# Attention plus expert-LoRA feed-forward block: value/LoRA column split 384 + 280, denominators in four column strips, token-stage order changed

## The chip, the cores and the metric

The kernel runs on one core of one Trainium2 chip. The metric is the device time of one execution in microseconds (us), lower is better; three runs of the kernel before are shown. The engines are named as in the profile: PE (TensorE), DVE (VectorE), ACT (ScalarE), POOL (GpSimd), SP (SyncE, which only issues DMAs here).

## What is computed

2048 tokens (2 x 1024) of width 512. After a layer norm, two branches are added to the input: linear attention and a gated feed-forward with routed low-rank experts.

```python
xn = layernorm(x)
# attention, 16 heads of 32
Q = elu(xn @ wq.T + bq) + 1;  K = elu(xn @ wk.T + bk) + 1;  V = xn @ wv.T + bv
KV = einsum('bhsd,bhse->bhde', K, V);  K_sum = K.sum(over tokens)
att = (Q @ KV) / (Q . K_sum + 1e-8)            # per head
att = att @ wo.T + bo
# feed-forward: 8 experts, top 2, rank 8, hidden 1376
scores = sigmoid(xn @ W_router); top 2 of (scores + expert_bias); w = their scores / (their sum + 1e-8)
gate = xn @ W_gate + shared LoRA + sum_e w_e * (xn @ A_gate[e]) @ B_gate[e] / 8      # up: the same
out  = (silu(gate) * up) @ W_down + shared LoRA + weighted expert LoRAs
return x + att + out
```

## The kernel before, in words

Every product is made nearly exact by splitting each operand into a rounded high part and the remainder (`_h`, `_l`, type fp32r): `product` issues three matmuls, L1112 to L1114 (high x high, high x low, low x high). Each engine has its own program, written out by hand; the order on an engine is the order of the code, and semaphores are the only link. `tiles` peels the first two and the last two tiles and puts the others into a loop of two tiles per turn.

**Token stage** (16 tiles of 128 tokens, `stage1` on each engine). On PE, for tile t: keys (512 columns, into bank 1), transposes of the normalised tokens of tile t+1 (L1129), transposes of the LoRA rows of tile t-2 (L1147), values (512 columns), then the low-rank inputs and router logits z (152 columns: 64 + 64 expert columns, 8 + 8 shared, 8 router), then keys by values of tile t-1 (L1139, accumulated over two tiles). Twelve matmuls make each of the three products of a tile. DVE, ACT and POOL work the tile up:

- layer norm of tile t+2: DVE statistics (L795, L799), POOL `rstd_of` (L508, L510), DVE `normalise` (xn, L804);
- keys: DVE bias (kb, L866), ACT krelu and kexp (L627, L630), DVE kf (L878);
- routing of tile t-1: ACT rexp (L642), POOL 1 + exp (L529), DVE `compare` (score, biased, gt, eq, L827 to L834), POOL ranks (L532 to L536), DVE `select` (sel, L839), POOL the sum, its inverse and the weights (L539 to L545);
- LoRA rows of tile t-1: DVE `lora_weighted` (zs, zf, L845, L849), ACT `lora_hi` (zst), DVE `lora_lo` (zst, L791);
- z of tile t: DVE copy out of the bank (zraw, L890), which has one buffer; every second tile DVE adds the keys-by-values bank (kvacc, L816).

POOL's loop is `rstd_of(t + 2)` and then `route(t)`, so the rstd of tile t+2 stands behind the routing of tile t-1. The output weight `wo` is split into high and low in tiles 14 and 15, two quarters each.

**Attention stage** (4 groups of 512 tokens): queries, `denominators` (L1223), DVE adds 1e-8 and takes the reciprocal (L964, L966), the reciprocals are split into `rr` and spread over the head's columns by a matmul with `hrow` (`expand`, L1231), and the attention matmuls follow. `denominators` is four matmuls in full fp32, one per 128 columns of Q, each with a 128 x 16 stationary tile `kcur` (key sums, zero off the head's own column); the four accumulate into the same 16 rows of a bank. DVE builds `ksel` once (L1001), POOL copies a batch's part into `kcur` (L565). Rows 0 to 15 of `rr` hold the high parts, rows 32 to 47 the low parts.

**Feed-forward stage** (4 groups x 11 chunks): gate, up and down products. The change does not touch it.

## Time and profile before

| | before |
|---|---|
| median of 3 runs | 725.01 us (724.76 to 725.21) |
| the profiled execution | 723.72 us |
| its span in the trace | 721.9 us |
| PE / PE weight loads busy | 98% / 79% |
| DVE / ACT / POOL busy | 53% / 36% / 17% |
| granted TensorE clock, mean | 1.00 |
| HBM traffic | 72.8 MB, 101 GB/s over the span |

A busy share is an average over three stages with different limits: the token stage lies at about 9 to 150 us of the span, the attention stage at 150 to 262 us, the feed-forward behind it. The start of an instruction is recorded; the end of a matmul is modelled, so consecutive matmuls overlap on paper and their rate is read from start to start.

### The profile page before, as it was taken

To read this page: it belongs to the slowest core of one execution; us is meant where nothing else is said; L and a number is where in the kernel's file an instruction comes from. 1 tells how busy PE (TensorE), PEld (TensorE's weight loads), DVE (VectorE), ACT (ScalarE), POOL (GpSimd) and SP (SyncE) were. 2 spreads that over 40 slices of the span, in tenths; PEclk is the share of its full clock that TensorE was granted. 3 is DMA by queue.
4 is the path that set the end of the run, shared out by engine and by line. 5 is a ranking of instruction groups with operands and counts; after the bars stand their busy time and mean duration, and the time that the engine had idled before them with its cause. 6 is when DMAs were issued, how large, how long until landed. Compare 5 with 4: busy or idle time off the path is not lost.

```text
span 721.9 us, 10024 instructions
## 1 busy us (share of the span) xinstructions
PE 706.6 (98%) x3306; PEld 570.8 (79%) x3306; DVE 380.2 (53%) x715; ACT 260.8 (36%) x402; POOL 123.1 (17%) x293
## 2 busy tenths in 40 slices
PE   7999999998999999999999999999999999999997
PEld 5888888876776767888888888888888888888886
DVE  5666655677666665444336543436534435544434
ACT  4343333563431432333324333324332324323322
POOL 3544455421633632000000000000000000000000
PEclk9999999999999999999999999999999999999999
DMA  7765556235755644100001600001600001300001
GB/s 248 276 199 195 185 189 220 88 146 195 287 183 206 214 166 172 63 0 0 0 11 48 233 0 0 0 0 58 232 0 0 0 0 58 116 0 0 0 0 59
DMA packets 22754, 73.03 MB, mean 101 GB/s; under 512 B 2560, under 2 KB 2816, under 8 KB 20688
## 3 DMA queue, kind: packets, MB, share of 16 engines
q1 hardware_dynamic: 22560, 72.50, 28.3%
q0 software_dynamic: 176, 0.30, 0.3%
q8 instruction: 10, 0.16, 0.1%
q14 instruction: 8, 0.07, 0.0%
HBM read 51.82 MB, written 20.97 MB: 101 GB/s over the span
## 4 chain that ended last, share of the span: by engine, by line
PE 88%; DVE 5%; issue 2%; POOL 2%; ACT 1%; DMA 1%; SPq 0%; DVEq 0%; POOLq 0%
PE bank L1112 18%; PE bank L1113 18%; PE bank L1114 18%; PE bank L1323 17%; PE bank L1298 6%; PE bank L1310 4%; PE bank L1223 2%; PE bank L1139 1%; PE bank L1175 1%; DMA w_raw<-in_wkT 1%; PE bank L1129 1%; PE bank L1147 1%; PE bank L1231 1%; PE bank L1339 0%; PE bank L1341 0%
## 5 line engine op out<-in xcount | busy, mean ns | idle before, releaser
L1112 PE MATMUL bank<-x,up_h 128*128 (+1 forms) x352 | 137.5, 391 | 2.1 <-DVE qf L977 1.2
L1113 PE MATMUL bank<-x,up_h 128*128 (+1 forms) x352 | 137.2, 390 | 0.0
L1114 PE MATMUL bank<-x,up_l 128*128 (+1 forms) x352 | 137.0, 389 | 0.0
L1045 DVE TENSOR_TENSOR hf<-bank,silu 128x512 f32<-128x512 f32 x44 | 30.4, 692 | 162.3 <-issue 142.6
L1112 PEld LDWEIGHTS bank<-x,up_h 128*128 128x128 f32 x352 | 66.1, 188 | 18.7 <-issue 2.1
L595 ACT ACTIVATE hid_h<-hf 128x512 fp32r<-128x512 f32 x44 | 27.8, 632 | 142.9 <-DVE hf L1045 142.9
L1114 PEld LDWEIGHTS bank<-x,up_l 128*128 128x128 f32 x352 | 66.1, 188 | 14.0
L1113 PEld LDWEIGHTS bank<-x,up_h 128*128 128x128 f32 x352 | 66.1, 188 | 13.8
L791 DVE TENSOR_TENSOR up_l<-up_raw,up_h 128x1024 fp32r<-128x1024 f32 x45 | 55.6, 1235 | 31.4 <-ACT up_h L595 31.4
L1323 PE MATMUL bank<-dn_h,hid_h 128*128 128x512 f32 x176 | 69.5, 395 | 0.0
L1323 PE MATMUL bank<-dn_l,hid_h 128*128 128x512 f32 x176 | 69.1, 393 | 0.0
L1323 PE MATMUL bank<-dn_h,hid_l 128*128 128x512 f32 x176 | 68.9, 392 | 0.0
L595 ACT ACTIVATE up_h<-up_raw 128x1536 fp32r (+1 forms) x45 | 66.0, 1474 | 1.5 <-DVE qf L946 1.5
L748 ACT ACTIVATE silu<-bank 128x512 f32<-128x512 f32 x44 | 26.3, 597 | 101.7 <-PE bank L1298 101.5
L1298 PE MATMUL bank<-z,up_h 128*128 128x512 f32 x176 | 54.2, 389 | 0.0
L791 DVE TENSOR_TENSOR hid_l<-hf,hid_h 128x512 fp32r<-128x512 f32 x44 | 30.5, 692 | 33.8 <-ACT hid_h L595 33.8
L595 ACT ACTIVATE dn_h<-dn_raw 128x592 fp32r (+1 forms) x44 | 30.8, 699 | 43.0 <-PE bank L1310 31.4
L791 DVE TENSOR_TENSOR up_h<-up_raw,up_h 64x256 fp32r<-64x256 f32 x90 | 39.5, 439 | 0.6
L791 DVE TENSOR_TENSOR dn_l<-dn_raw,dn_h 128x592 fp32r<-128x592 f32 x44 | 34.1, 775 | 10.4 <-ACT dn_h L595 9.3
L1323 PEld LDWEIGHTS bank<-dn_h,hid_l 128*128 128x128 f32 x176 | 33.0, 188 | 7.6
L1323 PEld LDWEIGHTS bank<-dn_h,hid_h 128*128 128x128 f32 x176 | 33.0, 187 | 7.5
L1323 PEld LDWEIGHTS bank<-dn_l,hid_h 128*128 128x128 f32 x176 | 33.1, 188 | 7.1
(167 smaller groups left out, 1252.6 us busy)
## 6 DMA issues: line engine op xcount, KB each, us to landing
x<-scr_x SPq DMA_DIRECT2D x8, 2048.0 KB, 7.4
up_raw<-in_ffn_up SPq DMA_DIRECT2D x11, 768.0 KB, 5.4
scr_x<-xt SPq DMA_DIRECT2D x16, 512.0 KB, 4.2
xin<-in_x SPq DMA_DIRECT2D x16, 256.0 KB, 5.8
scr_z<-zt SPq DMA_DIRECT2D x16, 256.0 KB, 2.2
x3r<-in_x SPq DMA_DIRECT2D x16, 256.0 KB, 4.0
scr_att<-x3r SPq DMA_DIRECT2D x16, 256.0 KB, 2.1
z<-scr_z SPq DMA_DIRECT2D x4, 1024.0 KB, 4.8
```

The source lines that it names most:

```text
L595: return nc.scalar.activation(dst, src, ACT.Copy)
L748: nc.scalar.activation(silu[:], ps_g[:], ACT.Silu).then_inc(silu_done, 1)
L791: return nc.vector.tensor_tensor(dst, a, b.bitcast(F32), ALU.subtract)
L1045: nc.vector.tensor_tensor(hf[:], ps_u[:], silu[:], ALU.mult).then_inc(h_done, 1)
L1112: nc.tensor.matmul(dst, lh, rh, start=start, stop=False, **kw)
L1113: nc.tensor.matmul(dst, lh, rl, start=False, stop=False, **kw)
L1114: return nc.tensor.matmul(dst, ll, rh, start=False, stop=stop, **kw)
L1129: last = nc.tensor.transpose(ps_xt[:, k * P:(k + 1) * P], xn[:, k * P:(k + 1) * P], ident[:])
L1223: last = nc.tensor.matmul(ps_den[0:HEADS, :], kcur[:, c, :], qf[:, c, :], start=(c == 0), stop=(c == KD - 1))
L1298: last = nc.tensor.matmul(dst[:], up_h[:, s, col:col + P], z4[:, :, a * 2 + b, :], start=False, stop=(b == 1))
L1310: d = nc.tensor.matmul(ps_zd[0:DNR, :], w[:, s, D:], h[:, s, :], start=(first and i == 0), stop=(last and i == 2), skip_group_check=True)
L1323: d = nc.tensor.matmul(ps_out[j][:], h[:, s, cols], w[:, s, 0:D], start=(first and i == 0), stop=False, skip_group_check=True)
```

## The change

Four parts.

1. **384 + 280.** The value weight and the z weight stand side by side in one array of 664 columns (`va_h`, `va_l`). The values' first 384 columns make one product (`va`), the last 128 value columns and the 152 z columns the other (`vz`, 280 columns). ACT copies the values in two pieces, and the last piece waits for DVE's `zraw` copy. PE waits for `va_done` before a `va` product and for `vf_done` before a `vz` product.
2. **Column strips.** `denominators` writes each of its four matmuls to 32 rows of its own (16 with the 4 heads' sums in high place, 16 the same again), each with `start` and `stop`. `kcur` is 128 x 32 per matmul, made by POOL from `hcol` and `kvacc`. `ksel` goes.
3. **LoRA-row layout of `rr`.** The strips hold every sum twice; DVE's reciprocal works on all 128 rows, ACT rounds all, and one DVE instruction turns the upper half of each strip into the low part with the mask `lomask` (-1 there, 0 elsewhere). The clearing of `rr` goes.
4. **Order in the token stage.** On DVE, `compare(t - 1)` moves behind the key bias kb of tile t, `select(t - 1)` behind the statistics, and `zraw(t)` ahead of `lora_weighted(t - 1)` and `lora_lo(t - 1)`; `zraw` has two buffers. On ACT, rexp comes ahead of `lora_hi(t - 1)`. `wo` is split one quarter a tile in tiles 12 to 15, for which `tiles` peels four last tiles in place of two.

```diff
-WO_HALF = {TILES - 2: (0, 1), TILES - 1: (2, 3)}
+WO_PART = {TILES - KD + k: k for k in range(KD)}
...
 # POOL
             def key_sums(g):
                 wait(pool, den_ready, g)
-                nc.gpsimd.tensor_copy(kcur[:], ksel[:, bass.ds(g // GB, 1)].rearrange("p o k n -> p (o k) n")
-                                      ).then_inc(kcur_done, 1)
+                sums = kvacc[:, bass.ds(g // GB, 1), :, P:AUG].rearrange("p o k n -> p (o k) n")
+                tt(kcur[:], hcol[:], sums.to_broadcast([P, KD, DK]), ALU.mult).then_inc(kcur_done, 1)
...
 # ACT
-                act.wait_ge(v_ready, t + 1)
-                round_to(vf[:, s, :, 0:P], ps_v[:].rearrange("p (k n) -> p k n", n=P)).then_inc(vf_done, 1)
+                act.wait_ge(va_ready, t + 1)
+                round_to(vf[:, s, 0:KD - 1, 0:P], ps_va.rearrange("p (k n) -> p k n", n=P)).then_inc(va_done, 1)
+                act.wait_ge(zraw_done, t + 1)
+                round_to(vf[:, s, KD - 1, 0:P], ps_vz[:, 0:P]).then_inc(vf_done, 1)
+                nc.scalar.activation(rexp[:], zraw[:, s, NZ - E:], ACT.Exp, scale=-1.0).then_inc(rexp_done, 1)
                 if behind(t, 1):
                     lora_hi(t - 1)
-
-                act.wait_ge(zraw_done, t + 1)
-                nc.scalar.activation(rexp[:], zraw[:, NZ - E:], ACT.Exp, scale=-1.0).then_inc(rexp_done, 1)
...
 # DVE
             def stage1(t, half, s):
                 first = isinstance(t, int) and t == 0
+                dve.wait_ge(k_ready, t + 1)
+                wait(dve, kf_done, t)
+                nc.vector.tensor_tensor(kb[:], ps_k[:], bk_b[:], ALU.add).then_inc(kb_done, 1)
                 if not first:
                     compare(t - 1)
-                    select(t - 1)
-
-                dve.wait_ge(k_ready, t + 1)
-                nc.vector.tensor_tensor(kb[:], ps_k[:], bk_b[:], ALU.add).then_inc(kb_done, 1)
                 if first:
                     tokens_lo(1, 1)
                 if ahead(t, 2):
                     stats_of(t + 2, s, half + 1)
...
+                if not first:
+                    select(t - 1)
 
                 dve.wait_ge(kexp_done, t + 1)
                 nc.vector.scalar_tensor_tensor(kf[:, s, :], kb[:], 0.0, kexp[:], ALU.max, ALU.add).then_inc(kf_done, 1)
...
-                if not first:
-                    lora_weighted(t - 1)
                 if ahead(t, 2):
                     normalise(t + 2, s)
+                dve.wait_ge(vz_ready, t + 1)
+                nc.vector.tensor_copy(zraw[:, s], ps_z).then_inc(zraw_done, 1)
                 if not first:
+                    lora_weighted(t - 1, 1 - s)
                     lora_lo(t - 1)
-                dve.wait_ge(z_ready, t + 1)
-                nc.vector.tensor_copy(zraw[:], ps_z[:, 0:NZ]).then_inc(zraw_done, 1)
                 if s == 0 and not first:
                     key_values(t - 1, half - 1)
...
-                nc.vector.tensor_scalar(den[0:HEADS, :], ps_den[0:HEADS, :], EPS, None, ALU.add).then_inc(dene_done, 1)
+                nc.vector.tensor_scalar(den, ps_den[:], EPS, None, ALU.add).then_inc(dene_done, 1)
...
-                sub(rr[DK:DK + HEADS, :], den[0:HEADS, :], rr[0:HEADS, :]).then_inc(rr_done, 1)
+                nc.vector.scalar_tensor_tensor(rr[:], rr[:].bitcast(F32), lomask[:], den, ALU.mult, ALU.add
+                                               ).then_inc(rr_done, 1)
...
-                nc.vector.tensor_tensor(ksel[:, b], hcol[:], kvacc[:, b, :, P:AUG].to_broadcast([P, KD, HEADS]), ALU.mult
-                                        ).then_inc(ksel_done, 1)
...
-            nc.vector.memset(rr[:].bitcast(F32), 0.0).then_inc(rr_clear, 1)
...
 # PE
-                wait(pe, vf_done, t)
-                tile_of(ps_v[:], s, wv_h, wv_l, split_before=KD if first else None).then_inc(v_ready, 1)
+                wait(pe, va_done, t)
+                tile_of(ps_va, s, va_h[:, :, 0:VA], va_l[:, :, 0:VA], split_before=KD if first else None
+                        ).then_inc(va_ready, 1)
...
-                wait(pe, zraw_done, t)
+                wait(pe, vf_done, t)
...
-                tile_of(ps_z[:, 0:NZ], s, a_h, a_l).then_inc(z_ready, 1)
+                tile_of(ps_vz, s, va_h[:, :, VA:], va_l[:, :, VA:]).then_inc(vz_ready, 1)
...
-                    last = nc.tensor.matmul(ps_den[0:HEADS, :], kcur[:, c, :], qf[:, c, :], start=(c == 0), stop=(c == KD - 1))
+                    last = nc.tensor.matmul(ps_den[c * DK:(c + 1) * DK, :], kcur[:, c, :], qf[:, c, :], start=True, stop=True)
```

How the instructions stand now. First DVE, one tile t of the loop in the token stage, the kernel before (score to eq and sel are the routing of tile t-1, zs, zf and zst its LoRA rows, xn is tile t+2):

```order
L827 RECIPROCAL score<-rden_106 128x8
L834 TENSOR_TENSOR eq<-biased 128x64
L839 SCALAR_TENSOR_TENSOR sel<-rank,score 128x8
L866 TENSOR_TENSOR kb<-bank,bk_b 128x512
L795 BN_STATS stats<-xin 128x6
L878 SCALAR_TENSOR_TENSOR kf<-kb,kexp 128x512
L791 TENSOR_TENSOR xt<-bank,xt 128x512
L849 TENSOR_TENSOR zf<-zraw,wtok 128x64 x2
L804 TENSOR_SCALAR xn<-xin,mv,rstd 128x512
L791 TENSOR_TENSOR zst<-zf,zst 128x2x64
L890 COPY zraw<-bank 128x152
```

The same tile of the same loop on DVE in the changed kernel:

```order
L869 TENSOR_TENSOR kb<-bank,bk_b 128x512
L833 RECIPROCAL score<-rden_103 128x8
L840 TENSOR_TENSOR eq<-biased 128x64
L801 BN_STATS stats<-xin 128x6
L845 SCALAR_TENSOR_TENSOR sel<-rank,score 128x8
L884 SCALAR_TENSOR_TENSOR kf<-kb,kexp 128x512
L797 TENSOR_TENSOR xt<-bank,xt 128x512
L810 TENSOR_SCALAR xn<-xin,mv,rstd 128x512
L892 COPY zraw<-bank 128x152
L855 TENSOR_TENSOR zf<-zraw,wtok 128x64 x2
L797 TENSOR_TENSOR zst<-zf,zst 128x2x64
```

kb now heads the tile, with compare and select behind it, and xn and zraw stand ahead of zf and zst. The small instructions between these rows (biased, gt, the two of the statistics, zs, the second zst) moved with their neighbours.

On PE in the attention stage's first group, before (the four denominator matmuls, between products of the output matrix M):

```order
L1114 MATMUL bank<-wo_h,kvt_l 128x512
L1223 MATMUL bank<-qf,kcur 16x512 x4
L1112 MATMUL bank<-wo_h,kvt_h 128x512
```

and in the changed kernel:

```order
L1115 MATMUL bank<-wo_h,kvt_l 128x512
L1225 MATMUL bank<-qf,kcur 32x512 x4
L1113 MATMUL bank<-wo_h,kvt_h 128x512
```

The place is the same; each of the four writes 32 rows, and their own 32, where all four wrote the same 16.

## Rows read from the trace of the kernel before

**Rows 1.** The page, part 1: busy time, share and instructions of each engine.

```profile
PE 706.6 (98%) x3306; PEld 570.8 (79%) x3306; DVE 380.2 (53%) x715; ACT 260.8 (36%) x402; POOL 123.1 (17%) x293
```

**Rows 2.** The page, part 4: the chain that ended last, by engine.

```profile
PE 88%; DVE 5%; issue 2%; POOL 2%; ACT 1%; DMA 1%; SPq 0%; DVEq 0%; POOLq 0%
```

**Rows 3.** Busy time by stretch: token stage, attention stage.

```profile
core 0: us, PE busy (x) PEld busy (x) DVE busy (x) ACT busy (x) POOL busy (x), PEclk, DMA share, GB/s
16.00:150.00 134.00, 132.90 (x802) 115.99 (x800) 83.98 (x285) 55.83 (x126) 66.00 (x223) 1.00 0.59 203
152.00:262.00 110.00, 107.86 (x458) 77.98 (x459) 77.51 (x105) 40.94 (x67) 39.32 (x40) 1.00 0.53 194
```

**Rows 4.** Timeline of PE, one tile: start, duration (us), instruction; firsts of each product.

```profile
44.95 0.48 PE L1112 MATMUL bank<-wk_h,xt 128*128 128x512 f32 x1
...
47.82 0.60 PE L1129 MATMUL bank<-ident_sb,xn 128*128 128x128 f32 x4
...
48.62 0.47 PE L1112 MATMUL bank<-wv_h,xt 128*128 128x512 f32 x1
...
51.48 0.23 PE L1112 MATMUL bank<-a_h,xt 128*128 128x152 f32 x1
...
52.78 1.10 PE L1139 MATMUL bank<-vf,kf 128*128 128x129 f32 x8
53.63 0.48 PE L1112 MATMUL bank<-wk_h,xt 128*128 128x512 f32 x1
```

**Rows 5.** Waits in 20 to 160 us: who waited for whom, total, times, longest.

```profile
DVE sel L839 <- POOL rank L536: 26.1, 15, 1.7
```

**Rows 6.** Timeline of DVE, one tile of the loop; in brackets idle before.

```profile
71.44 0.69 DVE L816 TENSOR_TENSOR kvacc<-kvacc,bank 128x516 f32 x1 [0.68 <-PE bank L1139]
72.16 0.20 DVE L827 RECIPROCAL score<-rden 128x8 f32<-128x8 f32 x1
...
74.70 0.17 DVE L839 SCALAR_TENSOR_TENSOR sel<-rank,score 128x8 f32<-128x8 f32 x1 [1.73 <-POOL rank L536]
74.78 0.68 DVE L866 TENSOR_TENSOR kb<-bank,bk_b 128x512 f32<-128x512 f32 x1
75.38 0.68 DVE L795 BATCH_NORM_STATS2 stats<-xin 128x6 f32<-128x512 f32 x1
...
78.04 0.17 DVE L845 TENSOR_SCALAR zs<-zraw 128x16 f32<-128x16 f32 x1
78.11 0.35 DVE L849 TENSOR_TENSOR zf<-zraw,wtok 128x64 f32<-128x64 f32 x2
78.39 0.55 DVE L804 TENSOR_SCALAR xn<-xin,mv,rstd 128x512 f32<-128x512 f32 x1
79.14 0.29 DVE L791 TENSOR_TENSOR zst<-zf,zst 128x128 fp32r<-128x128 f32 x1 [0.20 <-ACT zst L595]
...
79.43 0.31 DVE L890 COPY zraw<-bank 128x152 f32<-128x152 f32 x1
```

**Rows 7.** Timeline of POOL, the same tile, and a sum step of tile 14.

```profile
75.49 0.20 POOL L541 TENSOR_TENSOR ssum<-ssum 128x1 f32<-128x1 f32 x1
...
77.03 0.55 POOL L545 TENSOR_TENSOR wtok<-sel,ssum 128x8 f32 x1 [0.18 <-POOL ssum L544]
...
77.81 0.55 POOL L510 TENSOR_TENSOR rstd<-vare,mhalf 128x1 f32<-128x1 f32 x1
...
145.72 0.62 POOL L541 TENSOR_TENSOR ssum<-ssum 128x1 f32<-128x1 f32 x1
```

**Rows 8.** Timeline of PE and DVE, tile 1: the last key matmul, the key bias.

```profile
20.75 0.39 PE L1114 MATMUL bank<-wk_h,xt 128*128 128x512 f32 x1
...
24.10 0.68 DVE L866 TENSOR_TENSOR kb<-bank,bk_b 128x512 f32<-128x512 f32 x1
```

**Rows 9.** Timeline of DVE: tile 15's key bias, first instruction of the attention stage.

```profile
145.01 0.68 DVE L866 TENSOR_TENSOR kb<-bank,bk_b 128x512 f32<-128x512 f32 x1
...
150.94 0.69 DVE L791 TENSOR_TENSOR kvt_l<-bank,kvt_h 128x512 fp32r<-128x512 f32 x1 [0.76 <-ACT kvt_h L595]
```

**Rows 10.** Timeline of PE: the denominators of group 1, merged (eight records).

```profile
197.69 3.61 PE L1223 MATMUL bank<-qf,kcur 128*16 128x512 f32 x8
```

More of the change, by code:

```diff
@@ L34 @@
 HEADS, DK = 16, 32
+HC = P // DK
+LO = DK // 2
 E, R = 8, 8
@@ L40 @@
 NZ = 2 * ER + 2 * R + E
+NV = D + NZ
+VA = 3 * P
 AUG = P + 1
@@ L113, in program @@
         m_l = at("m_l", [P, BATCH, KD, D], F32R)
-        ksel = at("ksel", [P, BATCH, KD, HEADS])
         hrow = at("hrow", [P, KD, P], F32R)
@@ L120, in program @@
         end_at = place[0]
-        kcur = at("kcur", [P, KD, HEADS])
+        kcur = at("kcur", [P, KD, DK])
         rr = at("rr", [P, GN], F32R)
         x3r = at("x3r", [P, GT, D])
+        hcol = at("hcol", [P, KD, DK])
+        hcol_at = place[0] - 4 * KD * DK
         place[0] = m_l_at
@@ L129, in program @@
         hmask = at("hmask", [P, P])
-        hcol = at("hcol", [P, KD, HEADS])
         hrow_raw = at("hrow_raw", [P, KD, P])
@@ L133, in program @@
         bv_b = at("bv_b", [P, D])
+        assert place[0] <= hcol_at
         place[0] = base
@@ L171, in program @@
         earlier = at("earlier_sb", [P, E, E])
-        zraw = at("zraw", [P, NZ])
+        zraw = at("zraw", [P, 2, NZ])
         rexp = at("rexp", [P, E])
@@ L341, in tiles @@
             body(1, 0, 1)
-            with eng.Fori(0, TILES // 2 - 2) as p:
+            with eng.Fori(0, TILES // 2 - 3) as p:
                 body(2 * p + 2, p + 1, 0)
                 body(2 * p + 3, p + 1, 1)
-            for t in range(TILES - 2, TILES):
+            for t in range(TILES - 4, TILES):
                 body(t, t // 2, t % 2)
@@ L393, in _ @@
             stage1(0, 0)
-            for dst, name in ((hmask, "headmask"), (hcol, "headcol"), (hrow_raw, "headrow"), (bdn_raw, "b_dn")):
+            for dst, name in ((hmask, "headmask"), (hcol, "headcol"), (hrow_raw, "headrow"), (lomask, "lomask"), (bdn_raw, "b_dn")):
                 sp.dma_start(dst[:], dram[name]).then_inc(s2_in, 16)
@@ L998, in _ @@
             queries(0, (1,))
-            for b in range(BATCH):
-                nc.vector.tensor_tensor(ksel[:, b], hcol[:], kvacc[:, b, :, P:AUG].to_broadcast([P, KD, HEADS]), ALU.mult
-                                        ).then_inc(ksel_done, 1)
-            lora_weighted(TILES - 1)
+            lora_weighted(TILES - 1, (TILES - 1) % 2)
             lora_lo(TILES - 1)
```

69 lines of the change are left out of this document (36 added, 33 removed).

## The prediction

> **What bounds the kernel now.** I read the page first, then the stretches, then one tile of the token stage on each engine in order of time, since the change moves instructions there. PE is busy 98% [rows 1] and is 88% of the chain that ended last [rows 2]; in the token stage it is busy 132.9 of 134 us, in the attention stage 107.9 of 110 us, both at a granted clock of 1.00, so 2.4 GHz [rows 3]. On the page this is a kernel bound by matmuls, so fewer PE cycles should be time won one for one.
>
> A tile in the token stage says how much of that holds. PE takes 8.68 us from key product to key product (44.95 to 53.63): keys 2.87, transposes 0.80, values 2.86, z 1.30, keys by values 0.85 [rows 4]. DVE is not busy, but waits 1.7 us in each of 15 tiles for POOL's ranks [rows 5], and in the whole loop of two tiles it waits for PE only once, 0.68 us ahead of kvacc [rows 6]. The rest of its 17.36 us is a chain that closes on itself without PE: compare, ranks on POOL, select, sums on POOL, rstd on POOL, xn, zraw, rexp, compare. So this chain needs (17.36 - 0.68) / 2 = 8.34 us a tile, 0.34 less than PE. **PE binds by a hair**, and what the new order does to this chain counts for more than its busy share says.
>
> **Part 1, 384 + 280.** Twelve 512-column matmuls start in 2.86 us, 238 ns each, of which 512 / 2.4 = 213 ns stream columns; twelve of 152 columns take 1.30 us, 108 ns each, of which 63 stream [rows 4]. The trace has neither 384 nor 280 columns. Above, a straight line through both points gives the same sum as now: no gain. Below, bare streaming gives 160 + 117 = 277 ns in place of 346, 0.83 us a tile. I take streaming plus the 25 ns that 512 shows: 185 + 142 = 327 ns, 0.23 us a tile, because both new widths stream longer than the 108 ns at which the narrow product goes. The two ends stay for the rival in which PE binds. The Trainium skill (TensorE: Matmul & The Clock Gate, Back-to-back issue gap) gives columns / 2.4 plus 2.5 ns, by which the pair would be 282 ns and the gain 0.77 us a tile; it would also put 512 columns at 216 ns, and the trace disagrees with its 238.
>
> **Part 4, the order on DVE.** I add up the new loop from kb of tile t to kb of tile t+1, each piece start to start:
>
> - kb to compare: 0.60 (74.78 to 75.38, what kb holds DVE) [rows 6].
> - compare to select, with POOL's ranks between: 2.54 (72.16 to 74.70) [rows 6]. The statistics now run inside this wait (0.60 plus two small ones) and cost nothing.
> - select to xn: 3.69 (74.70 to 78.39) [rows 6], which is POOL's sums and weights until 77.58, then rstd until 78.36 [rows 7]. kf and xt lie inside it. It is unchanged because POOL still has rstd behind the routing.
> - xn to zraw: 0.47 (0.55 less the 0.08 by which kb's successor started ahead of its end), zraw to zs: 0.23 in the same way.
> - zs to the end of zf: 0.42 (78.04 to 78.46); from there over ACT to zst: 0.68; two zst: 0.29 (79.14 to 79.43) [rows 6]. Before, xn filled this wait; now nothing does.
>
> Sum 8.92 us. What left the loop is rexp and POOL's rden (about 0.9); what entered is kb (0.6) and the LoRA rows behind zraw (1.4, of which only 0.75 was open before). Every second tile kvacc adds 0.72 (71.44 to 72.16) [rows 6]. One piece can stretch: POOL's sum step took 0.62 instead of 0.20 in tile 14 while DVE worked on two SBUF operands [rows 7]; kf, such an instruction, now starts exactly with the sums. I take 0.1 a tile; the ends are 0 and 0.4. That is about 9.4 us a tile against PE's 8.68 before and 8.45 after: **DVE and POOL would bind the token stage**, and part 1 is worth nothing there.
>
> From kb of tile 1 to kb of tile 15 it is 120.9 us now (24.10 to 145.01) [rows 8, 9]. New: 13 tiles x 9.02 = 117.3; seven kvacc of 0.70 = 4.9; tile 14 has no xn but the head masks, 3.14 + 0.09 + 1.20 + 1.75 + 0.23 + 0.42 + 0.68 + 0.29 = 7.8 (1.75 is an estimate for the masks: an instruction of 512 columns holds DVE 0.60, and four of 128 somewhat more together). Together 130.0, **+9.1 us**.
>
> At the front it wins: kb of tile 1 stood behind select of tile 0 and started at 24.10, though its last key matmul began at 20.75 and ended at 21.14 [rows 8]. Now kb goes ahead; vz is longer than z by about 0.4 where PE is early, so kb starts near 21.5: **-2.6 us**.
>
> At the end it loses: from kb of tile 15 to kvt_l it was 5.93 (145.01 to 150.94) [rows 9]. Now the routing of tile 14 starts behind that kb: 0.60 + 2.54 to select, 3.0 to 3.5 to the weights, 0.42 for zs and zf, 0.5 for ACT's zst, 0.6 for kvt_h: about 7.9. **+2.0 us**. The quarter of `wo` (0.6) lies inside the wait for ranks.
>
> **Parts 2 and 3, the strips.** Eight records in 3.61 us, the last modelled at 0.59: 3.02 / 7 = 0.43 us from start to start, 3.44 for a group [rows 10]. So each fp32 matmul is two passes, one behind the other. The trace shows no two matmuls of different strips, so the gain is bounded: nothing if they queue as now; 3.44 - 0.86 = 2.58 a group if all four run side by side. I take the case between: records start in program order, the second pass of a strip must wait for its first, and the next strip's first pass runs beside it: 5 passes of 0.43 in place of 8, 1.29 a group, x 4 = **-5.2 us**. All of it counts: in groups 1 to 3 PE is the bound, and the reciprocal chain on DVE starts earlier by as much as the attention matmuls that cover it; in group 0 that chain itself is the path. DVE's instructions keep their 512 columns and go from 16 to 128 rows; I cost this at nothing. `ksel` lay ahead of a wait for POOL's weights and the clearing of `rr` behind the last query step: nothing. `kcur` as a multiply of 128 x 128 on POOL ends before the last query step in group 0 and has 2 us of room later: nothing, 0.3 us if not. One more small load, and a `hcol` twice as wide, stand early in SP's queue behind the first tile: nothing.
>
> **Sum.** -2.6 + 9.1 + 2.0 - 5.2 = +3.3 us. The profiled execution took 723.72, 1.3 below the median, and would become 727.0; against the median, 725.01 + 3.3 = **728.3 us**. A measurement can tell about 0.2% (1.45 us) from no change.
>
> **The rivals.**
> - *Strips side by side.* All four at once, -10.3 in all: 8.5 - 10.3 = -1.8, 723.2 us. For it: the strips share neither output rows nor a stationary tile. Against: the two passes of one matmul stand ahead of the next in one queue. The Trainium skill (the same page, Measured speedup vs the span model) reports three column tiles 2.38 times as fast; this one-pass figure would make 3.44 into about 1.45, -8.0 in all. No row here shows it.
> - *Strips queue as before.* Nothing won: 725.01 + 8.5 = 733.5 us. This is also the case in which this part doesn't do what its form suggests. For it: a group's matmuls show no overlap today, though only because they share their rows. The Trainium skill (TensorEngine Tiling (Array Packing), Key Properties) says that a change of tiling mode drains the engine, which would eat part of any gain; the 16-row form may already pay it, and no run shows it.
> - *PE stays the bound.* Place: the loop in the token stage. If some wait that I took whole is shorter in the new order (POOL's sums, ACT's zst), the loop could fall under PE's 8.45. That is the point at which it turns, 0.8 us (0.9 with the stretch) below my sum. Price: 14 x 0.23 = 3.2 won, and -2.6 + 2.0 - 5.2 as above: -9.0, 716.0 us; with bare streaming, 8 less. Against: each piece of the sum is a measured distance, and DVE and POOL run alone in it.
>
> **How the numbers follow.** Forecast 0.45, side by side 0.2, queueing 0.23, PE bound 0.12. Each carries about 2 us either way from the stretch and the tail. The range runs from 721.5 (side by side, low) to 736 (queueing, high) and leaves out the PE case and the far tails, 0.2. The forecast's own range is 726 to 731. Faster by over 0.2%: PE bound 0.12 and half of side by side, 0.22. Within: the other half and the forecast's lower tail, 0.19. Slower: 0.59.
>
> **What would show it.** Right: from kb to kb 9.0 and 9.7 us alternating on DVE; PE with idle time in the token stage, ended by xt or transposes that wait for xn; select still waiting for POOL; denominators in about 2.2 us a group; the feed-forward unchanged. Wrong: kb to kb at or under 8.5; PE without gaps; denominators at 0.9 or 3.4 us.

## The result and the profile after

The changed kernel took **731.02 us** (median of 5 runs, 728.72 to 731.6) against 725.01 before: ratio 1.008, 95% interval 1.0068 to 1.0092, so 6.0 us slower. The forecast was 728.3, with 721.5 to 736 as its range. The profiled execution has a span of 728.9 us (721.9 before) at a mean granted clock of 0.994. Its page, part 1 and the head of part 4, to be read against [rows 1, 2]:

```profile
PE 698.3 (96%) x3306; PEld 570.7 (78%) x3306; DVE 378.5 (52%) x712; ACT 261.6 (36%) x418; POOL 125.7 (17%) x293
...
PE 72%; POOL 9%; issue 9%; DVE 6%; ACT 2%; POOLq 1%; DMA 1%; SPq 0%; DVEq 0%; ACTq 0%
```

PE has 8.3 us less to do, and its share of the chain that ended last fell from 88% to 72%; POOL's rose from 2% to 9%. Marked at the same instructions in both traces, the 7.0 us between the spans fall into these stretches (us; the change is after minus before, the forecast what the prediction has for the stretch):

| stretch | before | after | change | forecast |
|---|---|---|---|---|
| start to kb of tile 1 | 24.10 | 21.18 | -2.9 | -2.6 |
| kb of tile 1 to kb of tile 15 | 120.91 | 134.31 | +13.4 | +9.1 |
| kb of tile 15 to kvt_l | 5.93 | 7.92 | +2.0 | +2.0 |
| kvt_l to denominators of group 0 | 19.90 | 20.92 | +1.0 | 0 |
| denominators of group 0 to those of group 3 | 80.31 | 73.15 | -7.2 | -3.9 |
| those to the last expansion | 9.21 | 8.38 | -0.8 | -1.3 |
| expansion to the first gate product that waits for qf | 5.93 | 7.43 | +1.5 | 0 |
| feed-forward | | | 0 | 0 |

The waits of the changed kernel between 20 and 165 us (who waited for whom; total us, times, longest) name the new loop:

```profile
ACT vf L602 <- DVE zraw L892: 65.6, 16, 4.9
POOL eq L539 <- DVE eq L840: 36.9, 15, 2.8
DVE xn L810 <- POOL rstd L517: 33.8, 14, 2.6
...
DVE sel L845 <- POOL rank L543: 14.0, 15, 1.5
```

DVE's wait for the ranks was 26.1 us [rows 5] and is 14.0, but a new wait of 2.5 us a tile, xn for POOL's rstd, costs 33.8. The timeline of DVE shows it, from one kb to the next (start, duration, instruction; in brackets the idle time before, with what ended it):

```profile
69.13 0.69 DVE L869 TENSOR_TENSOR kb<-bank,bk_b 128x512 f32<-128x512 f32 x1 [0.25 <-issue]
69.73 0.19 DVE L833 RECIPROCAL score<-rden 128x8 f32<-128x8 f32 x1
...
72.27 0.17 DVE L845 SCALAR_TENSOR_TENSOR sel<-rank,score 128x8 f32<-128x8 f32 x1 [0.81 <-POOL rank L543]
72.36 0.68 DVE L884 SCALAR_TENSOR_TENSOR kf<-kb,kexp 128x512 f32<-128x512 f32 x1
...
76.19 0.55 DVE L810 TENSOR_SCALAR xn<-xin,mv,rstd 128x512 f32<-128x512 f32 x1 [2.54 <-POOL rstd L517]
76.65 0.31 DVE L892 COPY zraw<-bank 128x152 f32<-128x152 f32 x1
76.87 0.17 DVE L851 TENSOR_SCALAR zs<-zraw 128x16 f32<-128x16 f32 x1
...
77.97 0.29 DVE L797 TENSOR_TENSOR zst<-zf,zst 128x128 fp32r<-128x128 f32 x1 [0.67 <-ACT zst L602]
...
78.27 0.68 DVE L822 TENSOR_TENSOR kvacc<-kvacc,bank 128x516 f32 x1
78.98 0.69 DVE L869 TENSOR_TENSOR kb<-bank,bk_b 128x512 f32<-128x512 f32 x1
...
88.47 0.69 DVE L869 TENSOR_TENSOR kb<-bank,bk_b 128x512 f32<-128x512 f32 x1 [0.24 <-issue]
```

The pitch is 9.85 and 9.49 us in turn, 9.67 a tile, where PE set 8.68 before [rows 4]. POOL in the same tile:

```profile
72.04 0.20 POOL L543 TENSOR_TENSOR rank<-gt 128x8 f32<-128x8 f32 x1
72.52 0.58 POOL L546 TENSOR_TENSOR ssum<-sel 128x4 f32<-128x4 f32 x1 [0.28 <-DVE sel L845]
73.18 0.19 POOL L547 TENSOR_TENSOR ssum<-ssum 128x2 f32<-128x2 f32 x1
...
75.60 0.55 POOL L517 TENSOR_TENSOR rstd<-vare,mhalf 128x1 f32<-128x1 f32 x1
```

And PE: the first matmul of `va`, of `vz`, the product behind them, then three whole lines elsewhere, a group's denominators, PE's wait ahead of the last expansion, and the first gate product that waits for qf:

```profile
69.34 0.42 PE L1113 MATMUL bank<-va_h,xt 128*128 128x384 f32 x1
...
71.53 0.29 PE L1113 MATMUL bank<-va_h,xt 128*128 128x280 f32 x1
...
73.08 1.05 PE L1140 MATMUL bank<-vf,kf 128*128 128x129 f32 x8
...
208.85 1.07 PE L1225 MATMUL bank<-qf,kcur 128*32 128x512 f32 x8
...
265.86 0.73 PE L1233 MATMUL bank<-rr,hrow 128*128 128x512 f32 x2 [1.64 <-DVE rr L974]
...
273.29 0.47 PE L1113 MATMUL bank<-x,up_h 128*128 128x512 f32 x1 [1.24 <-DVE qf L983]
```

Twelve matmuls of 384 columns take 2.19 us (182.5 ns each), twelve of 280 take 1.55 (129 ns): 3.74 in place of 4.16. The eight records of a group's denominators stand in 1.07 us, not 3.61 [rows 10].

Two losses have another cause. The granted clock, in stretches of 2 us (PE busy, instructions, clock, DMA share, GB/s):

```profile
162.00:164.00 2.00, 0.57 (x4) 1.00 0.12 46
164.00:166.00 2.00, 1.70 (x5) 0.60 0.00 0
166.00:168.00 2.00, 2.00 (x6) 0.54 0.34 131
...
264.00:266.00 2.00, 0.36 (x2) 1.00 0.02 6
266.00:268.00 2.00, 2.00 (x6) 0.70 0.37 138
268.00:270.00 2.00, 2.00 (x6) 0.50 0.33 124
```

0.50 is the 1.2 GHz level. Both times PE had just stood idle: 1.64 us ahead of the row at 265.86 above, and 1.82 us while it waited for `zst`:

```profile
163.43 0.66 PE L1148 MATMUL bank<-ident_sb,zst 128*128 128x128 f32 x4 [1.82 <-DVE zst L797]
```

Before, the longest idle time was 1.20 us at the first place (ahead of 151.89), and there was none at the second, and the clock stayed at 1.00. The whole +1.0 us from kvt_l to the denominators is the clock's. Run 2 below has the new `kcur` and no drop there and takes 19.89 us; run 4 has the old `kcur` and a drop and takes 20.87.

### The profile page after: what moved, and what is told of

Same layout as the page of the kernel before. It is cut to its first block, busy times and chain, and to the rows that moved or that the text cites. A ratio compares the mean times of both kernels' runs of the same rounds, so it can differ in the third digit from the quotient of the medians.

```text
span 728.9 us, 10012 instructions
## 1 busy us (share of the span) xinstructions
PE 698.3 (96%) x3306; PEld 570.7 (78%) x3306; DVE 378.5 (52%) x712; ACT 261.6 (36%) x418; POOL 125.7 (17%) x293
## 4 chain that ended last, share of the span: by engine, by line
PE 72%; POOL 9%; issue 9%; DVE 6%; ACT 2%; POOLq 1%; DMA 1%; SPq 0%; DVEq 0%; ACTq 0%
PE bank L1325 17%; PE bank L1113 14%; PE bank L1114 14%; PE bank L1115 14%; PE bank L1300 5%; PE bank L1312 4%; DVE qexp L971 1%; POOL ssum L551 1%; POOL gt L542 1%; POOL ssum L546 1%; POOL rstd L517 1%; POOL eq L539 1%; PE bank L1177 1%; DMA w_raw<-in_wkT 1%; POOL gt L540 1%
## 5 line engine op out<-in xcount | busy, mean ns | idle before, releaser
L797 DVE TENSOR_TENSOR hid_l<-hf,hid_h 128x512 fp32r<-128x512 f32 x44 | 30.5, 693 | 33.8 <-ACT hid_h L602 33.8
L1113 PE MATMUL bank<-va_h,xt 128*128 128x384 f32 (+1 forms) x128 | 41.9, 327 | 1.0 <-DVE va_l L797 0.8
L1115 PE MATMUL bank<-va_h,xt 128*128 128x384 f32 (+1 forms) x128 | 40.3, 315 | 0.0
L1114 PE MATMUL bank<-va_l,xt 128*128 128x384 f32 (+1 forms) x128 | 40.3, 315 | 0.0
```

The source lines that it names most:

```text
L797: return nc.vector.tensor_tensor(dst, a, b.bitcast(F32), ALU.subtract)
L1113: nc.tensor.matmul(dst, lh, rh, start=start, stop=False, **kw)
L1114: nc.tensor.matmul(dst, lh, rl, start=False, stop=False, **kw)
L1115: return nc.tensor.matmul(dst, ll, rh, start=False, stop=stop, **kw)
```

## The experiments

Four questions: which part of the change costs and which wins (the first four runs); why the new loop is 9.67 and not 9.37; whether the strips overlap because they are strips; what the best version is. Each run's ratio is to the kernel before on the same chip.

**1. Only the orders put back.** VectorE's and ScalarE's order as before; division, strips, two row buffers and a quarter of the output weight a tile stay.

```diff
-                dve.wait_ge(k_ready, t + 1)
-                wait(dve, kf_done, t)
-                nc.vector.tensor_tensor(kb[:], ps_k[:], bk_b[:], ALU.add).then_inc(kb_done, 1)
                 if not first:
                     compare(t - 1)
+                    select(t - 1)
+
+                dve.wait_ge(k_ready, t + 1)
+                nc.vector.tensor_tensor(kb[:], ps_k[:], bk_b[:], ALU.add).then_inc(kb_done, 1)
...
-                if not first:
-                    select(t - 1)
...
+                if not first:
+                    lora_weighted(t - 1, 1 - s)
                 if ahead(t, 2):
                     normalise(t + 2, s)
-                dve.wait_ge(vz_ready, t + 1)
-                nc.vector.tensor_copy(zraw[:, s], ps_z).then_inc(zraw_done, 1)
                 if not first:
-                    lora_weighted(t - 1, 1 - s)
                     lora_lo(t - 1)
+                dve.wait_ge(vz_ready, t + 1)
+                nc.vector.tensor_copy(zraw[:, s], ps_z).then_inc(zraw_done, 1)
```

> The changed kernel with only the token stage's order put back: on DVE compare and select ahead of kb, and zraw last; on ACT rexp behind lora_hi. Division, strips, the second zraw buffer and one wo quarter a tile stay. Theory A (the new order lengthens the loop of DVE and POOL to 9.67 us a tile): kb to kb falls to about 8.4 us (PE would need 8.3), token stage about 15 us shorter than in the changed kernel, total about 716.5 us. Theory B (PE stalls because the last piece of the values now waits for zraw, ahead of the next vz product, whatever the order): stays within 2 us of the changed kernel, 729 to 731.

Measured: 714.61 us, ratio 0.9867 (0.985 to 0.9883). The order alone turns a kernel 9.5 us faster than before into one 6 us slower. kb follows kb in 8.31 and 8.46 us, 8.38 a tile.

**2. The strips alone**, on the kernel before.

```diff
-                    last = nc.tensor.matmul(ps_den[0:HEADS, :], kcur[:, c, :], qf[:, c, :], start=(c == 0), stop=(c == KD - 1))
+                    last = nc.tensor.matmul(ps_den[c * DK:(c + 1) * DK, :], kcur[:, c, :], qf[:, c, :], start=True, stop=True)
```

with all that hangs on it (`headcol`, `headrow`, `lomask`, `kcur`, the reciprocal over 128 rows).

> The kernel before with the column strips and the LoRA-row layout of rr alone. Both theories: denominators take about 1.07 us a group instead of 3.61, groups 1 to 3 start 2.3 to 2.4 us sooner after one another, the last one gives back about 1.5 to 3 us (DVE's weight split stands ahead of the denominators' bias add, and PE idles for rr), total about 718.5 us (717 to 720). If the strips' gain were tied to something else in the change: about 725.

Measured: 716.9 us, ratio 0.9897 (0.988 to 0.9913): 7.3 us won against the 724.16 on that chip, with the same 1.06 us a group. The strips are worth what the rival "side by side" said less some 3 us, most of it idle time and clock in the last group.

**3. The order alone**, on the kernel before: part 4 of the change as its diff shows it, with the two row buffers and the quarters of the output weight.

> The kernel before with the new order of the token stage alone (with the two zraw buffers and one wo quarter a tile), 512 + 152 columns and 16-row denominators as before. Theory A: kb to kb 9.4 to 9.7 us as in the changed kernel, total 736 to 739 us. Theory B: no division, so no such wait; 722 to 726 us.

Measured: 736.92 us, ratio 1.0176 (1.0159 to 1.0193), 12.8 us lost. In its trace kb starts at 21.98 in tile 1 and 155.97 in tile 15: 9.57 a tile, so the order is slow by itself, with the old products too.

**4. The division alone**, on the kernel before, with ScalarE's copy of the last values behind the copy of the LoRA rows (zraw), as in the change.

```diff
-                tile_of(ps_v[:], s, wv_h, wv_l, split_before=KD if first else None).then_inc(v_ready, 1)
+                tile_of(ps_va, s, va_h[:, :, 0:VA], va_l[:, :, 0:VA], split_before=KD if first else None
+                        ).then_inc(va_ready, 1)
...
-                tile_of(ps_z[:, 0:NZ], s, a_h, a_l).then_inc(z_ready, 1)
+                tile_of(ps_vz, s, va_h[:, :, VA:], va_l[:, :, VA:]).then_inc(vz_ready, 1)
```

> The kernel before with the 384 + 280 division alone, order as before. PE needs 0.42 us a tile less (8.26 instead of 8.68). Theory A: the loop of DVE and POOL, about 8.35 to 8.4 us, takes over, so about 0.3 us a tile is won and 0.1 stays idle: 720 to 723 us. Theory B: slower than before by several us, 730 or more.

Measured: 723.51 us over 10 runs, ratio 0.9989 (0.998 to 0.9999): 0.65 won, at the edge of what can be told, and less than the 1.2 to 4.2 us that theory A expected. The pitch is 8.31 and 8.46, 8.38 a tile. PE no longer binds (run 8 will show it at 8.22); the chain over DVE and POOL does, near the 8.34 that the prediction read from [rows 6]. In the loop theory A holds: PE starts the keys of tile 15 3.75 us sooner (136.68, before 140.43). Most of this is lost at the loop's end. The chain is further behind PE there, so kb of tile 15 starts only 1.6 us sooner (143.44, before 145.01), and PE waits for the last piece of the values, which ScalarE copies behind zraw:

```profile
149.07 1.98 PE L1145 MATMUL bank<-vf,kf 128*128 128x129 f32 x8 [3.58 <-ACT vf L600]
```

Behind this gap the clock falls to 0.50. kvt_l still starts 1.4 us sooner (149.54, before 150.94), the first denominators 0.4 (170.41, before 170.84).

The three parts add up to -7.3 + 12.8 - 0.65 = +4.9, measured together +6.0.

**5. rstd out from behind the sums.** The changed kernel, one thing moved on POOL.

```diff
+                if between is not None:
+                    between()
                 pool.wait_ge(sel_done, t + 1)
...
-            with pool.Fori(0, TILES - 2) as t:
-                rstd_of(t + 2)
-                route(t)
+            rstd_of(2)
+            with pool.Fori(0, TILES - 3) as t:
+                route(t, between=lambda: rstd_of(t + 3))
+            route(TILES - 3)
```

> The changed kernel with one thing moved on POOL: the reciprocal deviation of a tile (two instructions, about 0.8 us) is worked out between the ranks and the sums of the tile three before it, and not behind those sums. VectorE's, ScalarE's and TensorE's orders are those of the changed kernel. Theory A: the changed token stage is a closed loop over two engines: kb, compare, POOL's ranks, select, POOL's seven sums, POOL's variance and rstd, xn, zraw, kb, 9.67 us a tile in its trace; with the rstd taken out from behind the sums the loop is cut, since select to xn no longer contains the sums, and the pitch of kb falls to 8.4 to 8.6 us; over 14 tiles 15 to 17 us less, of which some 2 to 3 come back in what follows the last tile (the sums end later there): 715 to 719 us. Rival B: it is VectorE's own order, with the selection ahead of kf and the value copy ahead of the weighting, that makes a tile long, whichever instruction of POOL ends last: then POOL's sums hold lora_weighted in place of xn and at most POOL's own 0.8 us come off a tile where nothing else binds: pitch 9.0 to 9.5, 722 to 730 us.

Measured: 720.92 us, ratio 0.9955 (0.9938 to 0.9972); kb to kb 8.68 and 9.07, 8.87 a tile. That lies between the two theories: 10.1 of the 16.4 us to the old order are regained, not all. The timeline of DVE shows the wait that took over:

```profile
95.23 0.17 DVE L848 SCALAR_TENSOR_TENSOR sel<-rank,score 128x8 f32<-128x8 f32 x1 [0.92 <-POOL rank L543]
...
98.96 0.17 DVE L854 TENSOR_SCALAR zs<-zraw 128x16 f32<-128x16 f32 x1 [1.67 <-POOL wtok L554]
...
100.14 0.29 DVE L800 TENSOR_TENSOR zst<-zf,zst 128x128 fp32r<-128x128 f32 x1 [0.67 <-ACT zst L605]
...
100.76 0.69 DVE L872 TENSOR_TENSOR kb<-bank,bk_b 128x512 f32<-128x512 f32 x1 [0.24 <-issue]
```

xn no longer waits, and it and the row copy lie inside the wait for the sums; but the sums still stand between select and the weighting (3.73 us), and the weighting's way over ACT still stands ahead of kb. The distances kb to select 3.14, select to zs 3.73, zs to zst 1.18 and zst to kb 0.62 or 1.01 add up to the pitch. So rstd closed one ring, and behind it lies a second through `wtok`, 0.8 us a tile shorter.

**6, 7. The two moves one at a time.** In run 6 compare and select are back ahead of kb, and the row copy and ScalarE's exp stay where the change puts them; in run 7 it is the other way round.

> The changed kernel with compare and select put back ahead of kb; xn and the copy of the LoRA rows stay ahead of lora_weighted and lora_lo, and ScalarE's exp ahead of lora_hi. Theory A (closed loop over DVE and POOL): select is released at the tile's start again, one POOL rank chain (about 2.3 us) and kb's and the statistics' time fall out of the loop, but the sums with the rstd behind them still stand between select and xn (3.9 us), and lora_weighted follows after: pitch of kb 8.8 to 8.9 us, about 0.8 below the changed kernel's 9.67, so 718 to 722 us. Rival B (the moved comparison is the whole of the loss): pitch as in the old order, 8.31 and 8.46, 714 to 716 us.

> The run with only the orders put back (714.6 us), with kb alone moved ahead of compare, and select behind the statistics, as the change does; the weighting, xn, lora_lo and the copy of the LoRA rows keep the old order, as does ScalarE's exp. Together with the runs of the old order, of the row copy first alone (718.4) and of the change (731.0) this fills a square of two moves. Theory A: two moves close one loop together; select late costs 0.5 us a tile only where everything behind POOL's sums is ahead of the row copy, and in the old order of the rows lora_weighted and xn wait for the same sums in parallel with TensorE's vz: pitch of kb 8.4 to 8.6 us, kb(1) 2.6 us sooner, 2 us more after the last tile: 714 to 718 us. Rival B: the two moves add, so this one bears what the row copy first doesn't (731.0 - 718.4 = 12.6): 726 to 728 us, pitch 9.2.

Measured: 718.4 us (ratio 0.9917, 0.99 to 0.9933; pitch 8.57 and 9.12, 8.85 a tile) and 717.58 us (0.9907, 0.9883 to 0.9931; pitch 8.01 and 8.94, 8.48 a tile), each in the range of its theory A. The square is then:

| | rows in the old order | row copy ahead of the weighting |
|---|---|---|
| compare and select ahead of kb | 714.6 | 718.4 |
| kb ahead of compare, late select | 717.6 | 731.0 |

One move costs 3.8, the other 3.0, both 16.4: 9.6 us belong to neither alone (8.9 by the ratios, since the runs are from different chips). In the traces, from kb of tile 1 to kb of tile 15, the moves cost 5.4, 1.3 and 15.3 us: 8.7 belong to neither. What run 7 loses lies mostly behind the loop, where kvt_l comes 9.0 us after kb of tile 15 and not 5.5, as in run 1. Each move takes more than one instruction along (xn and ScalarE's exp with the row copy, the late select with kb); which of them counts was not separated.

In the changed kernel every piece lies in one ring in series. With the late select alone the weighting and its way over ACT run in the time that POOL needs for rstd: from xn to the next kb it takes 0.98 and 1.69 us in turn in run 7's trace, in place of 2.41 and 2.79:

```profile
79.90 0.18 DVE L852 TENSOR_SCALAR zs<-zraw 128x16 f32<-128x16 f32 x1 [1.58 <-POOL wtok L552]
...
80.85 0.55 DVE L811 TENSOR_SCALAR xn<-xin,mv,rstd 128x512 f32<-128x512 f32 x1 [0.45 <-POOL rstd L517]
...
81.83 0.68 DVE L870 TENSOR_TENSOR kb<-bank,bk_b 128x512 f32<-128x512 f32 x1
```

With the row copy first alone kb is outside the ring, and the sums begin before kf does: select to xn takes 3.70 and 3.79 us in turn in place of 3.92. Each of them alone thus goes only 0.1 and 0.5 us past the 8.38 of the old order (8.48 and 8.85), both together 1.3 (9.67).

**8. The copy one place forward.** The old order, in which only the copy of the LoRA rows passes `lora_lo`.

```diff
                 if ahead(t, 2):
                     normalise(t + 2, s)
-                if not first:
-                    lora_lo(t - 1)
                 dve.wait_ge(vz_ready, t + 1)
                 nc.vector.tensor_copy(zraw[:, s], ps_z).then_inc(zraw_done, 1)
+                if not first:
+                    lora_lo(t - 1)
```

> The old order on VectorE and ScalarE (as in the run with only the orders put back, 714.6 us) with one step of the change's idea kept: the copy of the LoRA rows out of PSUM stands ahead of lora_lo, while lora_weighted stays ahead of xn and compare and select ahead of kb. Two buffers for the rows, strips and division as changed. Theory A: there VectorE waited at lora_lo for ScalarE's lora_hi while TensorE's vz stood in the bank; a copy there costs nothing and gives the bank back about 0.3 us sooner: pitch 8.2 to 8.3 (8.31 and 8.46 before), 711.5 to 714 us. Rival B: POOL, which runs 6.0 us of instructions with gaps in a chain with VectorE, sets the pitch, and it stays 8.38: 714 to 715.5 us.

Measured: 709.79 us, ratio 0.9801 (0.9785 to 0.9818), pitch 7.73 and 8.70, 8.21 a tile: theory A, and 1.7 us better than its range. The excess lies behind the token stage, where tile 15's copy no longer stands behind tile 14's `lora_lo`. The last value product of run 1 and of this run:

```profile
147.48 1.13 PE L1141 MATMUL bank<-vf,kf 128*128 128x129 f32 x8 [2.93 <-ACT vf L602]
```

```profile
143.74 1.13 PE L1141 MATMUL bank<-vf,kf 128*128 128x129 f32 x8 [0.63 <-ACT vf L602]
```

After 2.93 us of idle time run 1 has matmuls of 512 columns at 0.43 us from start to start until 152.0; here they run at 0.23, and from kvt_l to the first denominators it takes 20.0 us in place of 20.9.

In this order PE sets the pitch again. Its products follow one another without a gap: keys 2.88, transposes 0.79, `va` 2.18, `vz` 1.56, keys by values 0.81, 8.22 us in all, in every tile from the second on. So a further move on DVE alone should not shorten this loop; none was tried.

**9. The last group's split of the up weights placed early.**

```diff
-                    attention(g - 1, (0, 1))
-                if then is not None:
-                    then()
+                    attention(g - 1, (0,))
+                    if then is not None:
+                        then()
+                    attention(g - 1, (1,))
```

> The run with the row copy ahead of lora_lo (709.8 us), and in the last group VectorE's split of the first up weights (2.0 us) placed between the first and the second attention sum, where VectorE waited 2.0 us for TensorE, and not behind the second, where the denominators' sum waited for it. Theory A: TensorE's idle time of 1.64 us ahead of the last group's expansion falls by what the split held the denominators, 1.0 us (denominators ready at 258.6, read at 260.2, in the changed kernel's trace; the second attention sum ends 0.9 us later than now): 708.4 to 709.2 us, 0.7 to 1.3 less. Rival B: the reciprocal's chain (0.7 + 3.35 + 0.7 us) is longer than the two output tiles that TensorE has in that time whatever stands ahead, or the weights split is needed sooner by TensorE: no change, 709.5 to 710.2.

Measured: 708.3 us, ratio 0.9779 (0.9764 to 0.9795). The medians differ by 1.5 us, and the intervals of runs 8 and 9 overlap; the trace decides. PE's wait ahead of the last expansion, in run 8 and then in run 9:

```profile
245.74 0.73 PE L1234 MATMUL bank<-rr,hrow 128*128 128x512 f32 x2 [1.64 <-DVE rr L975]
```

```profile
245.08 0.73 PE L1235 MATMUL bank<-rr,hrow 128*128 128x512 f32 x2 [0.62 <-DVE rr L976]
```

The idle time falls by the 1.0 us that was expected. In run 8's trace 1.64 us of idle time did not lower the clock, in the changed kernel's it did: expansion to gate product takes 5.81 us at clock 1.00 in run 8 (245.74 to 251.55) and 7.43 in the changed kernel. So a gap of this size costs 1.6 us more in some executions only: of the eight traces that have this gap of 1.64 us, three have the lower clock behind it (the changed kernel, runs 1 and 2) and five do not (runs 5 to 8 and 11). The difference of the medians isn't made by that alone. Executions with the same mean granted clock differ by 1.1 to 1.3 us on average too: 708.9 and 709.5 us in run 8 against 707.6 to 708.3 in run 9 at 0.999 or more, 710.1 and 710.9 against 709.2 and 709.4 at 0.997.

**10. All denominators in one strip.**

```diff
-                    last = nc.tensor.matmul(ps_den[c * DK:(c + 1) * DK, :], kcur[:, c, :], qf[:, c, :], start=True, stop=True)
+                    last = nc.tensor.matmul(ps_den[0:P if c == 0 else DK, :], kcur[:].rearrange("p k n -> p (k n)") if c == 0 else kcur[:, c, :],
+                                            qf[:, c, :], start=True, stop=True)
```

> The changed kernel with the four denominator products of a group written one after the other into rows from 0 of the bank, in place of four column strips: the first with all 128 columns of the key sums, the other three with 32 columns into the first 32 rows, each started afresh, so the sums over heads are not those of the reference (the denominators are left out in effect). Theory A: what made the eight records of a group take 1.07 us in place of 3.61 is that the four products lie in different strips of 32 columns and run beside one another; in one strip they run in series: 3.4 to 3.7 us a group and 2.4 to 2.6 us more per group over three loop groups and the last: 740 to 742 us (span 738 to 740). Rival B: they are fast because each is started and ended by itself, with no accumulation onto the one before: then 1.1 us a group stay and the time is 731.

Measured: 738.44 us (one run), and in the trace

```profile
212.13 3.71 PE L1225 MATMUL bank<-qf,kcur 128*128 128x512 f32 x8
```

Same number of matmuls, same flags, the same 32 columns in three of four: in series again, 0.43 us from record to record. In the changed kernel's group four records start at 208.85 to 208.87 and the other four at 209.30 to 209.32. Distinct strips are what makes them overlap; whether it is the columns or the output rows that must differ can't be told, since here the two go together. The time is 1.6 us under the expected range because the last group has no idle time then (expansion 9.40 us behind the denominators, with no wait ahead of it), and the clock stays up there.

The run also answers what the prediction left open, whether a change of the products' width costs something. From the second record of 128 columns to the first of 32 it takes 0.52 us in place of 0.43, and as much from the last of 32 to the next product of 128. The 16-row form of the kernel before shows the same 0.52 behind it and 0.32 in place of 0.23 ahead of it, as do the strips, so both pay about 0.09 us for each change and the strips nothing more.

**11. The best order without the division.** Run 8 with value and LoRA products as in the kernel before.

> The run with the row copy ahead of lora_lo (709.8 us) with the division taken back: value in one product of 512 columns and LoRA rows in one of 152, the rest (strips, two row buffers, a quarter of the output weight a tile, order) as there. Theory A: with VectorE's and POOL's loop at 8.2 us a tile TensorE binds again without the division: its stage then takes 4.16 us in place of 3.74 for these products and gives the row copy its data later: pitch of kb 8.6 to 8.7 us in place of 8.21, 5 to 7 us more over 14 tiles: 714.5 to 717 us. Rival B: the division is worth what it gave alone on the kernel before (0.7 us), in any order: 710 to 711 us.

Measured: 716.26 us, ratio 0.9887 (0.9871 to 0.9903), pitch 7.97 and 9.43, 8.70 a tile, which is PE's 8.68 of [rows 4]. DVE now waits for PE at the row copy of every second tile:

```profile
106.16 0.32 DVE L888 COPY zraw<-bank 128x152 f32<-128x152 f32 x1 [0.74 <-PE bank L1110]
```

So the division that won 0.65 us alone is worth 6.5 here (6.2 by the ratios), where PE binds with it (8.22) and without it (8.70).

**12. The first key sums early.** Run 9 with POOL's first `kcur` ahead of its wait for the down bias.

> The run with the early split of the up weights, and POOL's key sums of the first group worked out ahead of its wait for the down bias and not behind it. Theory A: TensorE waited 0.3 us longer for the first key sums than for the last query (POOL's multiply of 0.91 us began when ScalarE's bias split was done): 0.2 to 0.4 us below the run with the early split alone, at the edge of what the rounds can tell. Rival B: the group's chain behind (reciprocal, expansion) waits for m_l or another producer anyway: no difference.

Measured: 708.1 us, ratio 0.9773 (0.9759 to 0.9787): no difference from run 9 that could be told. The trace says why:

```profile
159.14 0.41 POOL L573 TENSOR_TENSOR kcur<-hcol,kvacc 128x128 f32<-128x128 f32 x1
159.22 0.36 DVE L852 TENSOR_SCALAR zs<-zraw 128x16 f32<-128x16 f32 x1 [0.72 <-POOL wtok L552]
...
164.41 1.06 PE L1227 MATMUL bank<-qf,kcur 128*32 128x512 f32 x8 [1.42 <-DVE qf L952]
```

PE no longer waits for kcur. But the multiply now lies beside DVE's `zs`, which takes 0.36 in place of 0.17 us, and the whole chain behind it to the last qf comes 0.2 us later: given back where it was won. Runs 9 and 12 are the fastest versions found, 17 us under the kernel before.

## Why the prediction was right, and where it was not

**The bound and the sign: right.** It said that PE binds by 0.34 us a tile and that the new order closes a longer loop over DVE and POOL. In the trace before, PE's key products are 8.68 us apart in every tile from the second on, run 4 shows the chain at 8.38 (read: 8.34), run 3 shows the order slow by itself, and the waits name rstd.

**Front and end: right.** -2.9 against -2.6, and +2.0 against +2.0.

**The loop, +9.1: 4.3 too small.** The mechanism holds; of its pieces kb to select is 3.14 as summed, xn to zraw 0.46 (0.47), zraw to zs 0.22 (0.23), zs to zst 1.10 (1.10), both `zst` 0.30 (0.29). Three terms were mis-sized:

- Select to xn was taken as 3.69 + 0.1 and is 3.92 (before, it is 3.69 and 3.79 in turn, of which the prediction read the first). POOL's first sum takes 0.58 in place of 0.20 us, in every tile, beside kf, an instruction of DVE with two SBUF operands: nearly the 0.4 that was taken as the far end. But the weights step behind the sums takes 0.20 in place of the 0.55 of [rows 7], so that 0.23 of it arrives at xn. The Trainium skill (SBUF — State Buffer, SBUF: two separate sides) says that one of the two engines then waits for the whole of the other's instruction. The trace agrees: the sum that starts 0.16 us behind kf ends 0.06 us behind it (73.10 and 73.04). 0.13 x 13 = 1.7 us.
- `zst` to kb was taken as back to back, 0.29. In tiles 3, 5, 7 and 9, where the loop over two tiles begins anew, it is 0.61 to 0.69 (87.85 to 88.47), and DVE has 0.24 us in which it waits for nothing that the profile shows. In tiles 11 and 13, behind which the tiles are written out and no loop begins, it is 0.30 and 0.29. With 0.06 at the loop's entry this makes 1.4 us. Before, DVE waited for POOL at this place, which hides such a gap:

```profile
80.30 0.20 DVE L827 RECIPROCAL score<-rden 128x8 f32<-128x8 f32 x1 [0.55 <-POOL rden L529]
```

- "The quarter of `wo` (0.6) lies inside the wait for ranks" holds for its place and not for its cost, which was put at nothing. Beside it one of POOL's steps ahead of the ranks takes 0.38 us longer (the two below 0.92 in place of 0.55 together), and kb to select is 3.52 in place of 3.14 in tiles 12, 13 and 14: 1.1 us.

```profile
139.19 0.66 DVE L797 TENSOR_TENSOR wo_l<-w_raw,wo_h 128x512 fp32r<-128x512 f32 x1
139.33 0.92 POOL L542 TENSOR_TENSOR gt<-gt 128x32 f32<-128x32 f32 x2
```

**The strips, -5.2: the step that failed.** The prediction took the case between the bounds, "the second pass of a strip must wait for its first, and the next strip's first pass runs beside it", 5 passes in place of 8, 1.29 us a group. Measured, all four run side by side: the four first passes start within 0.02 us, the four second passes 0.43 us later. The second pass does wait for its own first, but no strip waits for another. A group's records go from 3.61 to 1.07 us, and 7.16 / 3 = 2.4 us a group are won, near the 2.58 of the rival "side by side", which had been given 0.2. Of the prediction's own signs 1.07 is nearest to one of being wrong (0.9; right was 2.2). The reason given against that rival ("the two passes of one matmul stand ahead of the next in one queue") didn't hold up the matmuls of the other strips. What the three loop groups show is -7.2 in place of -3.9; the last group gave 0.8 in place of 1.3, because there DVE's 2.0 us of weight splitting held the denominators' bias, and its idle time then cost 1.5 in clock. "DVE's chain starts earlier by as much" was true in the loop and not in the last group. That DVE's instructions cost nothing more on 128 rows was right: the reciprocal of 512 columns takes 3.34 us on 16 rows and 3.35 on 128.

**The clock: not thought of.** Two drops to 1.2 GHz behind idle gaps that the change makes itself: 1.0 us and 1.5. They are no part of any term of the sum, nor of any rival.

**The errors cancel in part, which is luck**: loop +4.3, clock +2.5, strips -2.8, front -0.3 make +3.7 on a forecast of +3.3, against the traces' +7.0. With the strips as forecast the traces would differ by about 10 us.

**The division, worth nothing: right for this kernel, and for the right reason.** Its size on PE was 0.42 us a tile, not 0.23 (182.5 + 129 = 311.5 ns a pair in place of 327); bare streaming, 277, was too low as well. The Trainium skill's rule (TensorE: Matmul & The Clock Gate, Back-to-back issue gap) gives 282 ns, also too low: none of the four widths here follows it.

**kcur, nothing or 0.3 us: nothing.** The multiply does end 0.27 us behind the last qf in group 0 (184.28 and 184.01). But kvt_l to the denominators takes 19.89 us in run 2 and 19.90 before: the last qf ends 0.17 us sooner after kvt_l in run 2, where `ksel` no longer stands on DVE.

## What to carry to other kernels

Before reordering one engine, write its cycle down with the other engines' pieces in it and ask of each wait what is queued behind it: two moves that cost 3 to 4 us each cost 16 together, since each put its wait ahead of what the other needed. An edit's worth belongs to the bound it meets: the same division of columns won 0.65 us where DVE and POOL bound and 6.5 once PE did, so try a neutral edit again after the bound has moved. And when a stage's end leaves PE idle (1.6 to 3.7 us in these runs), look at the granted clock of what follows.

## What the runs showed of the hardware

- Four fp32 products of 32 output columns each in four column strips take 1.07 us where one behind the other takes 3.61 to 3.71, a factor of 3.4. The Trainium skill's measured table (TensorE: Matmul & The Clock Gate, Measured speedup vs the span model) has 2.38 for three strips; its model, one matmul's duration plus about 4 ns for each further one, comes nearer: with the two records of a product 0.43 us from start to start and the last modelled at 0.59, it gives an estimate of about 1.03 us.
- A change from products of 128 output columns to ones of 16 or 32, or back, costs about 0.09 us: 0.52 from start to start in place of 0.43 (run 10, and before).
- DVE's reciprocal of 512 columns takes as long on 128 rows (3.35 us) as on 16 (3.34).
- Start to start of fp32r matmuls at 2.4 GHz: 108 ns for 152 columns, 129 for 280, 182.5 for 384, 238 for 512. Not one straight line: 0.16 ns a column from 152 to 280, 0.51 from 280 to 384, 0.43 from there to 512.
- The clock fell to the 1.2 GHz level (0.43 us from start to start of 512 columns in place of 0.23) at idle times of PE of 1.80 us (run 5), 1.82 (changed kernel and run 10), 2.93 (run 1), 3.58 (run 4) and 3.68 (run 7), and in three of eight traces at 1.64; not at 1.41 (run 3), 1.20 (before) or 0.63 (run 8), nor at the 1.41 to 1.59 ahead of group 0's denominators in any trace. At 1.64 us the length of the gap doesn't decide.
- POOL's multiply of 128 x 128 took 0.41 us in run 12 beside a small DVE instruction and 0.85 to 0.92 in every other group, where DVE worked on 512 columns.
- A POOL sum of 128 x 4 takes 0.58 us in place of 0.20 when it starts just behind a DVE instruction of 512 columns with two SBUF operands (run 3 and the changed kernel), and 0.20 where it starts ahead of it (run 6).
